# Decoder layer on one core: last threshold without its clip, latent copies shared out in two tiles, new instruction lists

## What is computed

```
x = layernorm(x + attn(x))      # 8 heads of 128 over a memory of 256 rows, 3 steps
x = layernorm(x + xattn(x, ctx))  # 16 heads, latent attention over 64 context rows with rotary factors
x = layernorm(x + x @ (W * scale).T + bias)
```

```
for _ in range(3):
    scores = einsum('bhsd,hnd->bhsn', xi, K) * beta
    w = entmax15(scores)          # square(clip(scores/2 - tau, 0)), tau such that the sum is 1
    xi = einsum('bhsn,hnd->bhsd', w, V)
```

## Time and profile before

| | |
|---|---|
| median of three runs | 892.58 us (891.53 to 894.0) |
| the profiled execution: time / span | 891.69 us / 889.9 us |
| busy share of the span: PE, DVE, ACT, POOL | 92%, 87%, 83%, 55% |
| mean granted clock of PE | 0.975 |
| largest groups | DVE moments L816 376.7 us, PE scores L1257 352.9 us, ACT residuals L726 334.2 us |

### The profile page before, as it was taken

The page is one execution under the profiler, slowest core; times in us unless marked ns, Lnnn a source line. Parts: engine busy times, 40 slices in busy tenths (PEclk is TensorE's granted clock), DMA queues, the critical chain, the costliest instruction groups (busy, mean ns, idle before and its releaser), DMA issues.

```text
span 889.9 us, 18293 instructions
## 1 busy us (share of the span) xinstructions
PE 816.0 (92%) x5598; PEld 697.7 (78%) x5598; DVE 770.2 (87%) x1955; ACT 738.2 (83%) x1787; POOL 493.2 (55%) x2306
## 2 busy tenths in 40 slices
PE   7999998799999989999997999998999998998962
PEld 6878887588798878888876888787888877877751
DVE  4799998999999999989998999999899999996331
ACT  3599897989988999888899799989979899986420
POOL 4144446654565665676466656575675747765223
PEclk9999999899999989999999999999999999999986
DMA  8900120000000000000000000000000000000001
GB/s 279 212 1 1 37 72 4 12 5 7 1 1 1 2 1 1 1 3 1 26 0 1 11 13 1 1 2 1 2 22 2 1 20 1 8 1 1 2 1 33
DMA packets 24215, 17.63 MB, mean 20 GB/s; under 512 B 11760, under 2 KB 23536, under 8 KB 23856
## 3 DMA queue, kind: packets, MB, share of 16 engines
q1 hardware_dynamic: 23872, 16.13, 6.4%
q0 software_dynamic: 240, 0.27, 0.2%
HBM read 14.30 MB, written 2.10 MB: 18 GB/s over the span
## 4 chain that ended last, share of the span: by engine, by line
PE 52%; DVE 23%; ACT 15%; POOL 6%; issue 4%; DMA 0%; SPq 0%; POOLq 0%; DVEq 0%
PE banks L1257 20%; PE banks L1280 10%; DVE moments L816 9%; ACT work L726 6%; PE banks L1340 5%; PE banks L1268 5%; PE banks L1304 4%; DVE top L796 4%; PE banks L1128 3%; ACT work L717 3%; ACT work L738 2%; DVE work L836 2%; PE banks L1314 1%; ACT work L733 1%; PE banks L1332 1%
## 5 line engine op out<-in xcount | busy, mean ns | idle before, releaser
L816 DVE BATCH_NORM_STATS2 moments<-work 128x6 f32<-128x512 f32 x576 | 376.7, 687 | 8.0 <-ACT work L726 3.7
L726 ACT ACTIVATE work<-work,neg_u 128x256 f32<-128x256 f32 x768 | 334.2, 522 | 28.5 <-DVE neg_u L828 20.5
L1257 PE MATMUL banks<-weights_s,work 128*128 128x256 f32 x1536 | 352.9, 383 | 3.6 <-ACT work L717 2.4
L1257 PEld LDWEIGHTS banks<-weights_s,work 128*128 128x128 f32 x1536 | 286.8, 191 | 46.0 <-issue 7.0
L717 ACT ACTIVATE work<-banks,neg_low 128x256 f32<-128x256 f32 x384 | 155.9, 499 | 3.8 <-DVE neg_low L807 3.6
L948 POOL TENSOR_TENSOR resid_sum<-moments 128x8 f32<-128x8 f32 x144 | 30.3, 211 | 218.4 <-DVE moments L816 217.5
L796 DVE MAX8 top<-banks 128x8 f32<-128x256 f32 x384 | 140.6, 413 | 11.2 <-PE banks L1257 10.9
L1268 PE MATMUL banks<-ident,work 128*128 128x128 f32 x768 | 113.3, 283 | 21.1 <-ACT work L738 11.5
L738 ACT ACTIVATE work<-banks 128x512 f32<-128x512 f32 x192 | 113.6, 612 | 14.2 <-PE banks L1268 14.1
L1268 PEld LDWEIGHTS banks<-ident,work 128*128 128x128 f32 x768 | 90.4, 145 | 38.9 <-issue 20.4
L1280 PE MATMUL banks<-weights_s,work 128*128 128x256 f32 x512 | 115.9, 381 | 1.0 <-ACT work L738 1.0
(11 more groups left out here) (155 smaller groups left out, 1087.9 us busy)
## 6 DMA issues: line engine op xcount, KB each, us to landing
work<-in_L_xattn_Wo_dram SPq DMA_DIRECT2D x2, 1024.0 KB, 11.3
out_dram<-work SPq DMA_DIRECT2D x16, 128.0 KB, 1.8
work<-in_L_xattn_w_kc_q_dram SPq DMA_DIRECT2D x2, 768.0 KB, 5.5
rows<-in_L_xattn_Wq_dram SPq DMA_DIRECT2D x1, 1536.0 KB, 14.1
rows<-in_x_dram SPq DMA_DIRECT2D x1, 1536.0 KB, 6.9
work<-in_L_attn_Wq_dram SPq DMA_DIRECT2D x1, 1024.0 KB, 9.6
work<-in_L_attn_Wo_dram SPq DMA_DIRECT2D x1, 1024.0 KB, 14.3
work<-in_ctx_dram SPq DMA_DIRECT2D x32, 32.0 KB, 2.2
```

What stands on the lines that cost most here:

```text
L726: ins = nc.scalar.activation(q_resid[:, j, h, :], q_resid0[:, j, h, :], ACT.Relu, bias=small["neg_u"][:, j, h:h + 1])
L816: ins = nc.vector.bn_stats(moments[:, j, 2 * q:2 * q + 2, :].rearrange("p h k -> p (h k)"), r.rearrange("p h n -> p n h"))
L1257: ins = nc.tensor.matmul(ps_scores[:, h, :], lhsT, w[:, h, t, :], start=(t == 0), stop=(t == CT - 1))
```

## The change

Three things.

1. The clip after the last evaluation of a step is gone. The weights of DVE and ACT take POOL's `neg_u_raw` and wait for POOL's semaphore instead of DVE's. The clips after the first and second evaluation stay.
2. In tiles 14 and 15 (TAIL_TILES = 2) the second halves of `queries_out`, `probs_out` and `contexts_out` are DVE's instead of ACT's, and the second half of `normalise` is DVE's instead of POOL's. They count on a semaphore of their own (`half_emptied`), and PE waits for both.
3. All lists of turns are new. In them, the end of POOL's list is `15:normalise 0, worst_all, 15:rstd 1, 15:bias, 14:rstd 2, 15:rstd 2` (13:rstd 2 stands some places earlier, in front of 12:rstd 2), and the end of DVE's is `15:sum 1, 15:normalise 1, 14:residual 2, 15:probs_out 1, worst, 15:contexts_out 1, 15:residual 1, 15:norm 1, 15:residual 2, 14:norm 2, flag, 15:norm 2`, with 13:norm 2 and 12:norm 2 behind 15:queries_out 1. PE's list has the same stages; 377 of its 700 keep their place, and most others move by one or a few.

```diff
         for e in range(EVALS):
-            dve += four("moments", s, e) + once("inverse", s, e) + once("clip", s, e)
+            dve += four("moments", s, e) + once("inverse", s, e)
+            dve += once("clip", s, e) if e < EVALS - 1 else []
...
-    dve += once("residual", 0) + once("norm", 0) + two("shift") + two("sum")
-    dve += once("residual", 1) + once("norm", 1) + once("residual", 2) + once("norm", 2)
-    act += once("x_out") + two("queries_out") + two("exp") + two("probs_out") + two("contexts_out") + once("dense_in")
-    pool += once("rstd", 0) + two("normalise") + once("rstd", 1) + once("bias") + once("rstd", 2)
+    dve += once("residual", 0) + once("norm", 0)
+    dve_tail = dve + half("queries_out", 1) + two("shift") + two("sum") + half("normalise", 1) + half("probs_out", 1)
+    dve_tail += half("contexts_out", 1)
+    dve += two("shift") + two("sum")
...
+    act_tail = act + half("queries_out", 0) + two("exp") + half("probs_out", 0) + half("contexts_out", 0) + once("dense_in")
...
+    pool, pool_tail = pool + two("normalise") + after, pool + half("normalise", 0) + after
...
+            def last_threshold(eng, p, j, s):
+
+                eng.wait_ge(pool_step[j], pool_count(p, s, EVALS - 1, 11))
...
                     elif stage == "act_weights":
 
-                        act.wait_ge(u_ready[j], eval_count(p, s, EVALS - 1))
+                        last_threshold(act, p, j, s)
                         for h in pair:
                             ins = nc.scalar.activation(q_resid[:, j, h, :], q_resid0[:, j, h, :], ACT.Relu,
-                                                       bias=small["neg_u"][:, j, h:h + 1])
+                                                       bias=small["neg_u_raw"][:, j, h:h + 1])
...
                     elif stage == "weights":
-                        dve.wait_ge(u_ready[j], eval_count(p, s, EVALS - 1))
+                        last_threshold(dve, p, j, s)
...
+                    elif stage == "normalise":
+                        heads = slice(8 * q, 8 * q + 8)
+                        dve.wait_ge(soft_step[j], p * SOFT_PASS + (2 * q + 4))
+                        nc.vector.tensor_tensor(q_probs[:, heads, :], q_probs[:, heads, :],
+                                                q_inv[:, j, heads].unsqueeze(2).to_broadcast([P, 8, XD]),
+                                                ALU.mult).then_inc(soft_step[j], 1)
+                    elif stage == "probs_out":
+                        dve.wait_ge(lat_made[j], made(p, "turn_probs", q))
+                        nc.vector.tensor_copy(q_probs_t[:, 4 * q:4 * q + 4, :],
+                                              pq_pairs[:, 4 * q:4 * q + 4, :]).then_inc(half_emptied[j], 1)
```

More of the change, by code:

```diff
@@ L51 @@
 DVE_WEIGHTS = 2
+TAIL_TILES = 2
 def latent_head(at):
@@ L129, in __init__ @@
             tile = int(c, TILES + 2)
-            self.order.append((tile, stages[max(0, tile - TILES + 1)][at[c]]))
+            which = tile - TILES + 2 if tile >= TILES else int(tile >= TILES - TAIL_TILES)
+            self.order.append((tile, stages[which][at[c]]))
             at[c] += 1
@@ L151, in four, with half @@
         return [(name, s, e, q) for q in range(4)]
+    def half(name, q):
+        return [(name, 0, 0, q)]
     def once(name, s=0, e=0):
@@ L178, in tile_stages @@
     dve_out = once("mem_norm") + out[1][:3] + x_stats[:1] + out[1][3:11] + once("ffn_scale") + out[1][11:] + x_stats[1:]
-    return {"PE": [pe, [], made], "DVE": [dve, once("worst") + once("flag"), dve_out], "ACT": [act, [], out[0]],
-            "POOL": [pool, once("worst_all"), once("setup") + x_rstd + once("diag_zero")],
-            "SP": [once("fetch") + once("store"), [], []]}
+    sp = once("fetch") + once("store")
+    return {"PE": [pe, pe, [], made], "DVE": [dve, dve_tail, once("worst") + once("flag"), dve_out],
+            "ACT": [act, act_tail, [], out[0]],
+            "POOL": [pool, pool_tail, once("worst_all"), once("setup") + x_rstd + once("diag_zero")],
+            "SP": [sp, sp, [], []]}
@@ L552, in emptied, with in_tail, wait_emptied @@
                 return p * EMPTIED_PASS + EMPTIED[stage] + q
+            def in_tail(p, j):
+                return p * SLOTS + j >= TILES - TAIL_TILES
+            HALF = {"queries": 1, "turn_probs": 2, "contexts": 3}
+            TAIL_EMPTIED = {"turn_x": 2, "queries": 3, "turn_probs": 4, "contexts": 5, "turn_dense": 6}
+            def wait_emptied(eng, p, j, stage, q=0):
+                if not in_tail(p, j):
+                    eng.wait_ge(lat_emptied[j], emptied(p, stage, q))
+                elif q:
+                    eng.wait_ge(half_emptied[j], HALF[stage])
+                else:
+                    eng.wait_ge(lat_emptied[j], p * EMPTIED_PASS + TAIL_EMPTIED[stage])
             def read(p, stage, q=0):
@@ L1307, in run @@
                     elif stage == "scores_lat":
-                        pe.wait_ge(lat_emptied[j], emptied(p, "queries", 1))
+                        for half in range(2):
+                            wait_emptied(pe, p, j, "queries", half)
                         for bank in (6, 7):
@@ L1324, in run @@
                     elif stage == "contexts":
-                        pe.wait_ge(lat_emptied[j], emptied(p, "turn_probs", 1))
+                        for half in range(2):
+                            wait_emptied(pe, p, j, "turn_probs", half)
                         for bank in (6, 7):
```

114 lines of the change are left out of this document (68 added, 46 removed).

## The result

The changed kernel takes 881.08 us in the median of 4 runs (880.23 to 882.72), the kernel before, beside it, 893.29 (891.53 to 895.26). The ratio is 0.986, 95% interval 0.984 to 0.988: 12.2 us faster. Measured again later beside another run of the kernel before, it took 879.12 against 892.19, ratio 0.9864 [0.9844, 0.9883]. The forecast was 887.3 us, its range 883.5 to 895. So the sign was right and the gain was more than twice the one predicted, outside the range.

A forecast was written before the change was run, and what follows sets the result against it. The prediction took PE, with holes from late matrices, to bound the middle and one chain to bound the end. Terms -2.1 - 0.2 - 3.0, lists 0, gave -5.3 us: 887.3 us, range 883.5 to 895.

The forecast's parts named there:

- The clips: Removing 48 last clips from DVE: 1.8 us from DVE's time, 0.3 from ACT's shorter waits; -2.1 us, between 0 and -9.3.
- The halves: Tiles 14 and 15: DVE's query copy lets tile 15's latent scores begin earlier, -0.2 us; the other halves gain nothing.
- The end: Last tile: tile 13's rstd moves before the all-reduce and POOL's gaps run once it is free; variance 3.0 us sooner.
- Rivals 1 and 2: At the end, POOL's gap before the all-reduce starts only at `worst`: 893.6 and 890.4 us, chances 0.18 and 0.12.
- rival 1: At the end, both POOL gaps start only when their instruction's data is there: +1.0 us, 893.6 us, chance 0.18.
- The lists in the middle: New order of the middle: taken as 0, bounded at plus or minus 8.6 us by three windows' lower clock.
- rival 3: In the middle, new lists open two more PE holes at lower clock: +6.8 us, total 894.1 us, chance 0.22.
- The sum: Whole kernel: clips, halves and end added as -2.1 - 0.2 - 3.0 = -5.3 us, giving 887.3 us.
- Rival 4: The clip was never on the path, so only -3.2 us remains: 889.4 us, chance 0.06.

The follow-up runs named there:

- c4_clip_idle: Kernel before with its old lists and all 96 clips done, but weights take the raw threshold and wait for POOL: 891.07 us, -2.3 us.
- i1_clip_idle_newmid: h_ono with all 96 clips done on DVE, but weights still take the raw threshold and wait for POOL: 882.71 us, -9.5 us against before.
- c2_tail_new_end: Kernel before with the halves of tiles 14 and 15 on DVE and the new list end; clip kept, old order elsewhere: 890.47 us, -2.9 us.
- d0_all_old: Kernel before with 48 clips gone, halves on DVE and the new list end; old order everywhere else: 889.24 us, -3.0 us.
- h_ono: d0_all_old with the new order from 340 to 588 us and SP's new list: 881.75 us, -10.5 us against before.
- i2_clip_used_newmid: h_ono with all 96 clips done and waited for by the weights: 887.25 us, -5.0 us against before.
- t1_rstd13_behind: h_ono with tile 13's last rstd (POOL) and norm (DVE) put back behind the all-reduce: 883.43 us, ratio to before 0.9896.
- t_after: The changed kernel itself, measured again beside another run of the kernel before: 879.12 us, ratio 0.9864.

## Why the prediction fell short

**What bounds the kernel.** Right: PE's list with holes, and an end that is one chain. But the holes were looked for in three windows only. The ones at 160 and 320 kept their clock; the one at 480 moved to 450 to 480 with its clock, and the one that closed, at 540 to 580, was not among them.

**The clips, -2.1.** Right in size when alone (-2.0 and -2.3, clock included), wrong in its parts. It was worked out as DVE's time by DVE's share of the chain (1.8) and a shorter wait (0.3). `c4_clip_idle` and `i1_clip_idle_newmid` keep DVE's time and lose 1.0 us by it at most. A share of the chain says how often the path runs over an engine; it doesn't say that taking some instructions off that engine shortens the path by that share. (DVE's groups by form show the removal as forecast, 18.5 - 10.5 = 8.0 us:

```profile
L874 DVE TENSOR_TENSOR neg_u<-neg_u_raw,neg_limit 128x8 f32<-128x8 f32 x48 | 10.5, 219 | 2.0 <-POOL neg_u_raw L1038 1.5
```

It brought nothing by itself.) What can be said from the trace is who waits for the instruction: ACT's L733, 11.1 us, now 5.4. The prediction took 1.8 us off that wait and held the rest to be POOL's and DVE's chain; 5.7 went, with clip and order together.

**The halves, -0.2.** Seen as forecast: the scores wait 0.67 us for DVE's copy (L960) and for nothing else. DVE's product L965 took 0.84 us beside POOL's (853.12 to 854.16), and ended at 854.70, inside PE's turns (from 854.21, 2.06 long), whose first half takes POOL's. DVE's copies took 0.69, forecast 0.68.

**The end, -3.0.** The mechanism held. The disputed point was whether the two gaps of the earlier trace rows run from when POOL is free. `worst` was 2.93 us late against POOL's freedom, and the first gap was 5.62, not 2.93 + 5.83. Rivals 1 and 2 would have put the all-reduce at 857.09 + 5.83 = 862.92; it came at 859.78. In the traces of `c2_tail_new_end`, `d0_all_old`, `h_ono`, `i2_clip_used_newmid`, `t1_rstd13_behind` and `t_after` it also comes 5.55 to 5.88 us after POOL is free and only 2.6 to 3.0 after `worst`. Here the trace differs from what the prediction drew for rival 1 out of the Trainium skill, page GPSIMD Engine Reference, section 2.1 (Instruction dispatch): the size of about 6 us for the first call of a freshly loaded kernel agrees with the rows (5.55 to 5.88), but the time runs beside the wait and not behind it. Measured from tile 15's scores to its variance: 22.52 before, 848.25 to 866.80 = 18.55 after, 4.0 gained where 2.8 was in the sum (22.52 to 873.40 - 853.65 = 19.75). The missed 1.2: the first gap 0.2, the second, 6.64 for 7.43, 0.8, and POOL's normalise, which the sum left at its old time although the scores begin 0.2 earlier, 0.2. The part behind it, said to be unchanged at 13.5 us, took 12.7: 0.8 more.

**The lists in the middle, 0. This is the step that failed.** The term was set to 0 because no row prices it, and the chance was given to the slower side (rival 3, two new holes at lower clock). `h_ono` against `d0_all_old` shows -7.5 us for the order from 340 to 588 us in the kernel without the clip. The bounds of plus and minus 8.6 held that value, but the range did not follow them: it went down by one bad window (887.3 - 3.4 is 883.9; the text has 883.5). The bounds were also made of the wrong thing, time lost at lower clock. Between the same two PE stages the kernel before and the changed one both have 3.4 us at 1.2 GHz; what went is PE's idle time, 9.7 to 5.8 us, and 2 us of its busy time, 5.9 us together. The clock went only in some executions (none in `h_ono` and `t_after`, two stretches in `d0_all_old`), which is 3.4 of the 8.8 us between the traces of `h_ono` and `d0_all_old`.

**The sum.** The terms do not add. In the middle 2.1 and 0.1 gave 7.6, and by the traces, less the clock, 2.2 and nothing gave 5.2. A wait that is made shorter pays only where the order leaves nothing else to wait for behind it; which stages those are in the old order was not traced. That -2.0 and -2.9 gave -3.0 in the old order is not clear of the intervals. Rival 4 (the clip never on the path) fits the old order, where the stretch is 257.7 us with the clip and 257.9 without, less the clock, and is false of the new one.

What remains open is which exchanges between 340 and 588 us let the clip's absence count, and why an execution of one kernel has one stretch at 1.2 GHz more than another. Only the one tried, tile 7's evaluation behind tile 8's, is ruled out as sufficient.

## What to carry to other kernels

In a kernel whose order is written out, an edit that shortens a wait and the order made for it are one change: price them together, and give the order a range as wide as the holes it could close, on the fast side as well as on the slow. Price an instruction by who waits for it, not by its engine's share of the chain, and look at every window with PE under full, not at the worst few. Compare two orders between the same stages, not between the same times: a hole can leave its window and still be there. And before a clock is counted as the gain of an order, look at a second execution of the same kernel. The gap on GpSimd ahead of the all-reduce was hidden by setting the engine free early; the all-reduce's data could come 2.9 us later.

## What was not expected of the hardware

- The gap on POOL ahead of the all-reduce was 5.55 to 5.88 us in the eight traces named here, with `worst` ready before POOL was free (the kernel before) or 2.7 to 2.9 us after (the others). The gap behind it, from the all-reduce's end to the next ordinary product, was 6.64 to 7.43 in the four timelines quoted; the 6.64 ended 0.43 us after the product's data.
- Taking 8 us of work off VectorE, busy 87% of the span, moved the time by 1.0 us at most in both orders (891.37 to 891.07; 881.75 to 882.71).
- Runs of one kernel can fall in two groups: the kernel with the clip in the new middle took 883.24 once and 886.7 to 887.6 five times, the changed kernel 883.02 once and 878.66 to 879.48 four times. The odd one has a mean granted clock of 0.979 against 0.974 to 0.977 in the first case and 0.974 against 0.978 to 0.979 in the second, so the times go with the clock there. It is no fixed price: the four of `h_ono`, 0.977 to 0.982, lie within 0.7 us.
